# Images in DRAM with the two column parities side by side: blocks of columns in 2048-byte runs, blocks of rows in two DMAs

## The chip, the cores and the metric

The kernel runs on one core of a Trainium2 chip. The metric is the device time of one execution, from the first to the last instruction of the program, in microseconds (us). The time before is the median of three runs.

## The reference

Four layers work on images of 4 batches, 48 channels, 256 rows and 256 columns (float32). Each layer is `x = x + f(gn(x))`, where `gn` is a group norm with 16 groups of 3 channels.

```python
# layer 0
qkv = conv3x3_depthwise(conv1x1(gn(x), qkv_w), dw_w);  q, k, v = split(qkv)
x = x + conv1x1(softmax(l2n(q) @ l2n(k).T * temperature) @ v, proj_w)
# layers 1 and 2: four sweeps over the image, each one a chain of steps
D[t] = row[t] + conv1d(D[t-1], down_w)            # down, 256 steps
U    = the same weights, upwards over D           # up
R[t] = column[t] + conv1d(R[t-1], right_w)        # right
L    = the same upwards over R with left_w        # left
x = x + L
# layer 3
h = conv3x3_depthwise(conv1x1(gn(x), w_in), w_dw); x1, x2 = split(h)
x = x + filter_8x8_patches(conv1x1(gelu(x1) * x2, w_out), fft_w)
```

## The kernel before

An image (3,072 KB for each of 16 blocks, 48 MB in all) is stored in DRAM in sub-blocks. A block is 16 rows or 16 columns; a sub-block is the crossing of both, and it is stored by parity: `hp` is the parity of the row, `wp` that of the column, and 64 numbers (`SUB`) are left for one batch. The layout before is `[hb, wb, hp, wp, c, b, s]`: block of rows, block of columns, the two parities, channel, batch, the 64 numbers. One run of consecutive bytes for one channel is `(b s)`, 256 numbers or 1,024 bytes. This holds for the input `x` (the host writes it so) and for the four images `x1`, `x2`, `up` and `x3` between the layers.

In SBUF a block has 96 partitions, 48 channels times a parity, with 32 KB in each. For a block of rows (`row_block`) the partition is `(wp c)`, so the lower 48 partitions hold the even columns; for a block of columns (`col_block`) it is `(hp c)`. A block of rows is one DMA over all 96 partitions, 32 runs of 1,024 bytes in each. A block of columns is four DMAs, one for each `(hp, wp)`, over 48 partitions each, 16 runs of 1,024 bytes in each; first the two of partitions 0 to 47 (`hp` 0), then the two of 48 to 95. The phases of one batch (`RowStream`) load a block of rows of one batch in one DMA: 96 partitions, 32 runs of 256 bytes.

The phases follow each other with a barrier between them:

- `stats_phase` (st): loads the 16 blocks of rows of `x` into two tiles in turn, and VectorE takes their statistics. Nothing else runs. The load of block n + 2 is issued when VectorE is done with block n.
- `gram_phase` (qk), `value_phase` (va), `gated_phase` (gf): `RowStream` over 4 batches with 16 blocks of rows each. For each strip of 8 rows ScalarE writes `own_high`, GpSimd `own_low`, and SyncE (SP) issues two copies of each inside SBUF (`next_high`, `next_low`, one for 48 partitions each) that TensorE waits for. After every second strip SP issues the load of a later block; `value_phase` also stores a block of its result.
- `down_up_phase` (du, once for each of layers 1 and 2): blocks of rows in, the sweep down, lines stored; then the lines back in, the sweep up, blocks of rows out.
- `right_left_phase` (rl, twice): blocks of columns in, the sweep to the right, lines stored; then, going back for the sweep to the left, for each block: the lines in (3,072 KB), the block of the residual in, the block of the result out. In layer 2 ScalarE also writes the result again by patches (`repack`, L657), and SP stores it in eight DMAs a block (`store_patches`, L593). ScalarE may write a patch buffer again only when the store of two buffers before has landed (L663).
- `filter_phase` (fi).

All DMAs are issued by SP in the order in which its code is written, and they go through one queue. What waits for a load is written in semaphore counts: 16 for each DMA, so that `dve.wait_ge(loaded[k], 64 * i + 64)` waits for four.

Of the kernel before, what the change touches and what calls it, by code (L numbers as in the profile page):

```python
# [98 lines left out]
def stats_phase(nc, src, stats):  # L99

    with Phase(nc, "st") as ph:
# [5 lines left out]
        @block.sync  # L107
        def _(sp):
            for k in range(2):
                sp.dma_start(tiles[k][:, :].rearrange("p (k s) -> p k s", s=B * SUB),  # L110
                             row_block(src, k)).then_inc(loaded[k], 16)
            with sp.Fori(1, NB // 2) as i:
                for k in range(2):

                    ph.hold(sp, used, 2 * i + k - 1)
                    sp.dma_start(tiles[k][:, :].rearrange("p (k s) -> p k s", s=B * SUB),
                                 row_block(src, 2 * i + k)).then_inc(loaded[k], 16)
# [253 lines left out]
def down_up_phase(nc, src, taps, scale, shift, down, dst):  # L371
# [4 lines left out]
    with Phase(nc, "du") as ph:  # L376
# [13 lines left out]
        def _(sp):  # L390
            def load(n, k):
                sp.dma_start(wide[k][:, :].rearrange("p (k s) -> p k s", s=B * SUB), row_block(src, n))\
                  .then_inc(loaded[k], 16)
# [11 lines left out]
            def store_back(i, k):  # L405
                m = 2 * i + k
                ph.hold(sp, placed, BLK * m + BLK)
                sp.dma_start(row_block(dst, NB - 1 - m), wide[k][:, :].rearrange("p (k s) -> p k s", s=B * SUB))\
                  .then_inc(back_out[k], 16)
# [17 lines left out]
            for k in range(2):  # L427
                sp.wait_ge(back_out[k], 16 * (NB // 2))

        @block.scalar  # L430
        def _(act):
# [3 lines left out]
            def back(i, first=False):  # L435
                for k in range(2):
                    m = 2 * i + k
                    if not first:
                        act.wait_ge(back_out[k], 16 * i)
# [11 lines left out]
            with act.Fori(0, NB // 2) as i:  # L451
                for k in range(2):
                    act.wait_ge(loaded[k], 16 * i + 16)
# [80 lines left out]
def right_left_phase(nc, src, taps_right, taps_left, right, dst, residual, stats, patches=None):  # L534
# [4 lines left out]
    with Phase(nc, "rl") as ph:  # L539
# [16 lines left out]
        def pieces(t, n, tile):  # L556
            v4 = tile[:, :].rearrange("p (k q s) -> p k q s", q=2, s=B * SUB)
            return [(col_block(t, n, hp, wp), v4[hp * C:(hp + 1) * C, :, wp]) for hp in range(2) for wp in range(2)]

        @block.sync  # L560
        def _(sp):
            def load(n, k):
                for d, s in pieces(src, n, wide[k]):
# [5 lines left out]
            def load_residual(m):  # L569
                for d, s in pieces(residual, NB - 1 - m, results[m % 3]):  # L570
# [40 lines left out]
            for m in range(NB):  # L611
                if m >= 1:
                    store_back(m - 1)
                if m >= 2:
                    store_patches(m - 2, 3)
                    if m + 1 < NB:
                        sp.wait_ge(measured, m - 1)
                        sp.wait_ge(back_out[(m - 2) % 3], 64 * ((m - 2) // 3 + 1))
# [12 lines left out]
            for k in range(3):  # L631
                sp.wait_ge(back_out[k], 64 * len(range(k, NB, 3)))
# [56 lines left out]
        def _(dve):  # L689
            def there(i, first=False):  # L690
                for k in range(2):
                    n = 2 * i + k
                    dve.wait_ge(loaded[k], 64 * i + 64)
# [38 lines left out]
        def _(pool):  # L732
            def place(m, tile, count, first=False):
                pool.wait_ge(whole[tile], 64 * count + 64)
# [34 lines left out]
class RowStream:  # L769
# [83 lines left out]
    def norm(self, act, b, hb):  # L853
# [8 lines left out]
        self.ph.hold(act, self.raw_in[kr], 16 * self.loads_of(kr) * b + 16 * (hb // self.raws) + 16)  # L862
# [387 lines left out]
def value_phase(nc, src, scale, shift, w_v, dst, stats):  # L1250

    with Phase(nc, "va") as ph:
# [11 lines left out]
        def _(sp):  # L1264
            def store(b, hb):
                ph.hold(sp, added, 4 + NGB * b + 4 * (hb + 1))
                d = dst[hb][:, :, :, :, bass.ds(b, 1)].rearrange("wb hp wp c b s -> (wp c) (wb hp) (b s)")
                sp.dma_start(d, rs.raw[hb % 4][:, :].rearrange("p (k s) -> p k s", s=SUB)).then_inc(stored[hb % 4], 16)

            def before_load(b, hb):  # L1270
                if hb >= 2:
                    ph.hold(sp, stored[(hb - 2) % 4], 16 + 64 * b + 16 * ((hb - 2) // 4) + 16)
                    ph.hold(sp, measured, NB + NB * b + hb - 1)
                else:
                    ph.hold(sp, stored[hb + 2], 16 + 64 * b)
# [7 lines left out]
            for k in range(4):  # L1283
                sp.wait_ge(stored[k], 16 + 64 * B)
# [526 lines left out]
```

## Time and profile before

| | |
|---|---|
| median of 3 runs | 12107.07 us (12071.13, 12107.07, 12110.31) |
| profiled execution, its own time | 12072.02 us |
| its span | 12070.2 us |
| busy TensorE (PE) | 11062.8 us, 92% |
| busy VectorE, ScalarE, GpSimd | 7592.0, 3302.3, 5472.2 us |
| moved by DMA | 1907.40 MB, 1974004 packets |

PE is TensorE's matmuls and PEld its weight loads, DVE is VectorE, ACT ScalarE, POOL GpSimd; SPq, ACTq and so on are the sequencers of the engines, which issue DMAs and wait for semaphores. The profiled execution stands near the lowest of the three runs, 35 us below their median.

### The profile page before, as it was taken

What the parts mean: (1) busy time and instruction counts of PE and PEld (TensorE: products, weight loads), DVE (VectorE), ACT (ScalarE), POOL (GpSimd) and SP (SyncE); (2) the same over time, 40 slices, a digit from 0 to 9 for tenths busy, and PEclk for the clock granted to TensorE, in tenths of its full rate; (3) what the DMA queues carried; (4) which work ended last, traced back from release to release, by engine and by line L of the source; (5) the groups of instructions that cost most, each with busy time, mean ns of one, the idle gap of its engine ahead of it and who ended that gap; (6) DMA issues with size and microseconds to landing.
All of it is one profiled execution on the core that took longest, in us unless ns stands there. A gap on an engine that the chain in (4) does not pass through costs nothing. (4 is left out here: it accounts for less than half of the span.)

```text
span 12070.2 us, 242619 instructions
## 1 busy us (share of the span) xinstructions
PE 11062.8 (92%) x82492; PEld 10237.2 (85%) x82492; DVE 7592.0 (63%) x19405; ACT 3302.3 (27%) x3654; POOL 5472.2 (45%) x5025
## 2 busy tenths in 40 slices
PE   0999999899989998999899999999879999999999
PEld 0999999666669998998799889987779999999974
DVE  5444444322248886877778777866667676777754
ACT  0222222222222352023322450055622222222210
POOL 0666666333335554555455444544434444444410
PEclk9999999899999999999899999988889999999999
DMA  9666666699976567879765658799845555555569
GB/s 173 136 138 136 137 133 135 133 194 193 192 154 181 136 177 160 183 161 205 159 161 142 167 142 177 164 197 214 197 102 113 104 112 114 107 115 104 116 197 360
DMA packets 1974004, 1907.40 MB, mean 158 GB/s; under 512 B 1224122, under 2 KB 1863968, under 8 KB 1900960
## 3 DMA queue, kind: packets, MB, share of 16 engines
q1 hardware_dynamic: 1973152, 1897.01, 69.9%
q8 instruction: 417, 6.83, 0.2%
q14 instruction: 435, 3.56, 0.1%
HBM read 781.57 MB, written 578.81 MB: 113 GB/s over the span
## 5 line engine op out<-in xcount | busy, mean ns | idle before, releaser
L744 POOL TENSOR_TENSOR rl_wide<-rl_wide,rl_state 96x512 f32<-96x512 f32 x510 | 818.3, 1605 | 812.1 <-ACT rl_state L655 812.1
L273 PE MATMUL du_sum<-du_high,sw_down_high 96*96 96x256 f32 x6132 | 1085.8, 286 | 102.9 <-DVE du_high L335 75.7
L273 PE MATMUL du_sum<-du_low,sw_down_high 96*96 96x256 f32 x6132 | 1118.2, 291 | 0.1
L273 PE MATMUL du_sum<-du_high,sw_down_low 96*96 96x256 f32 x6132 | 1078.2, 284 | 0.0
L940 POOL TENSOR_TENSOR gf_own_low<-gf_sums,gf_own_high 96x2080 fp32r<-96x2080 f32 x128 | 598.5, 4676 | 901.4 <-DVE gf_hid_a L1520 896.4
L1436 PE MATMUL gf_four<-gf_own_high,l_w_hid_high 96*128 96x256 f32 x3072 | 883.8, 288 | 108.4 <-DMA gf_next_low<-gf_own_low 108.4
L273 PEld LDWEIGHTS du_sum<-du_high,sw_down_high 96*96 96x96 f32 x6132 | 831.9, 165 | 111.3 <-DVE du_high L335 78.8
L934 POOL TENSOR_TENSOR gf_sums<-gf_block 96x520 f32<-96x520 f32 x512 | 602.7, 1207 | 666.1 <-DVE gf_hid_a L1520 637.9
L940 POOL TENSOR_TENSOR qk_own_low<-qk_sums,qk_own_high 96x2080 fp32r<-96x2080 f32 x128 | 596.8, 4662 | 666.4 <-ACT qk_own_high L904 666.4
L1436 PE MATMUL gf_four<-gf_next_high,l_w_hid_low 96*128 96x256 f32 x3072 | 874.1, 285 | 0.0
L346 POOL TENSOR_TENSOR du_low<-du_state,du_high 96x128 fp32r<-96x128 f32 x1020 | 613.1, 601 | 573.2 <-DVE du_state L336 573.2
L1436 PE MATMUL gf_four<-gf_own_low,l_w_hid_high 96*128 96x256 f32 x3072 | 873.0, 284 | 0.0
L1436 PE MATMUL gf_four<-gf_next_low,l_w_hid_high 96*128 96x256 f32 x3072 | 872.9, 284 | 0.0
L1436 PE MATMUL gf_four<-gf_own_high,l_w_hid_low 96*128 96x256 f32 x3072 | 871.4, 284 | 0.0
L1436 PE MATMUL gf_four<-gf_next_high,l_w_hid_high 96*128 96x256 f32 x3072 | 871.4, 284 | 0.0
L346 POOL TENSOR_TENSOR du_low<-du_lines,du_high 96x128 fp32r<-96x128 f32 (+1 forms) x1024 | 614.9, 601 | 555.9 <-DVE du_lines L336 555.9
L346 POOL TENSOR_TENSOR rl_low<-rl_lines,rl_high 96x128 fp32r<-96x128 f32 (+1 forms) x1024 | 614.3, 600 | 550.4 <-DVE rl_lines L336 550.4
L273 PEld LDWEIGHTS du_sum<-du_high,sw_down_low 96*96 96x96 f32 x6132 | 831.9, 164 | 0.0
L273 PEld LDWEIGHTS du_sum<-du_low,sw_down_high 96*96 96x96 f32 x6132 | 796.1, 164 | 31.5 <-issue 0.8
L1155 DVE COPY qk_second<-qk_four 128x192 f32<-128x192 f32 x512 | 183.0, 357 | 1008.5 <-PE qk_four L1128 1008.5
L648 ACT COPY rl_sum<-rl_lines 96x512 f32<-96x512 f32 x510 | 304.5, 597 | 1846.3 <-PE rl_sum L282 1846.0
L449 ACT COPY du_wide<-du_state 96x512 f32<-96x512 f32 x510 | 626.4, 1228 | 558.7 <-DVE du_state L336 558.7
(214 smaller groups left out, 32209.2 us busy)
## 6 DMA issues: line engine op xcount, KB each, us to landing
qk_next_high<-qk_own_high SPq DMA_DIRECT2D x256, 389.8 KB, 5.2
qk_next_low<-qk_own_low SPq DMA_DIRECT2D x256, 389.8 KB, 5.3
gf_next_high<-gf_own_high SPq DMA_DIRECT2D x256, 389.8 KB, 5.4
gf_next_low<-gf_own_low SPq DMA_DIRECT2D x256, 389.8 KB, 5.5
du_wide<-x SPq DMA_DIRECT2D x32, 3072.0 KB, 17.0
up<-du_wide SPq DMA_DIRECT2D x32, 3072.0 KB, 20.9
rl_wide<-up SPq DMA_DIRECT2D x128, 768.0 KB, 15.8
rl_wide<-x SPq DMA_DIRECT2D x128, 768.0 KB, 16.5
```

The source lines that it names most:

```text
L273: mm = self.nc.tensor.matmul(self.half_line(r, c), w[0:kk, k, :], x[0:kk, (r - 1) % RING, 2 * c:2 * c + 2, k:k + PAIRS], start=(n == 0 and ...
L346: self.nc.gpsimd.tensor_tensor(self.low_of(r, 2 * c, nb), state[:, 0:nb], self.high_of(r, 2 * c, nb), ALU.subtract)\
L449: nc.scalar.copy(result(k, r), by_sub_block(state[:, (TURN + r) % DEPTH])).then_inc(placed, 1)
L648: nc.scalar.copy(ch.line(t), lines[n % 2][:, at].rearrange("p b n -> p (b n)")).then_inc(ch.filled, 1)
L744: nc.gpsimd.tensor_tensor(at, at, by_sub_block(row), ALU.add).then_inc(placed, 1)
L934: last = g.tensor_tensor(self.sums4[:, 4 * t:4 * t + 4, :], d[x], d[y], op)
L940: g.tensor_tensor(self.parts["own", "low"][u % SLOTS][:, :, :], rows, self.parts["own", "high"][u % SLOTS][:, :, :], ALU.subtract).then_in ...
L1155: nc.vector.tensor_copy(second[:, 0, :], m[2]).then_inc(mid, 1)
L1436: mm = nc.tensor.matmul(four[tile][t // 2][:, (t % 2) * HN:(t % 2 + 1) * HN], w[:, ab, t, 128 * tile:128 * tile + 128], px[:, 4 * t + 2 * ...
```

## The change

The layout in DRAM becomes `[hb, c, wb, hp, wp, b, s]`: the channel moves outwards, and the two column parities stand next to each other. A block of columns has then runs of `(wp b s)`, 2,048 bytes, and is moved in two DMAs, one for each half of the partitions. A block of rows can no longer be written as one pattern over `(wp c)`, and is moved in two DMAs, `wp` 0 into partitions 0 to 47 and `wp` 1 into 48 to 95, with runs of 1,024 bytes as before, 2,048 bytes apart; so are the blocks of one batch, with runs of 256 bytes. The semaphore counts follow. What stands in SBUF, and what the engines compute, is the same.

```diff
-def row_block(t, hb):
-    return t[hb].rearrange("wb hp wp c b s -> (wp c) (wb hp) (b s)")
-def col_block(t, wb, hp, wp):
-    return t[:, wb, hp, wp].rearrange("hb c b s -> c hb (b s)")
+def row_block(t, hb, tile):
+    v = tile[:, :].rearrange("p (k s) -> p k s", s=B * SUB)
+    return [(t[hb][:, :, :, wp].rearrange("c wb hp b s -> c (wb hp) (b s)"), v[wp * C:(wp + 1) * C]) for wp in range(2)]
+def row_part(t, hb, b, tile):
+    v = tile[:, :].rearrange("p (k s) -> p k s", s=SUB)
+    return [(t[hb][:, :, :, wp, bass.ds(b, 1)].rearrange("c wb hp b s -> c (wb hp) (b s)"), v[wp * C:(wp + 1) * C])
+            for wp in range(2)]
+def col_block(t, wb, tile):
+    v = tile[:, :].rearrange("p (k x) -> p k x", k=NB)
+    return [(t[:, :, wb, hp].rearrange("hb c wp b s -> c hb (wp b s)"), v[hp * C:(hp + 1) * C]) for hp in range(2)]
...
-                    sp.dma_start(tiles[k][:, :].rearrange("p (k s) -> p k s", s=B * SUB),
-                                 row_block(src, 2 * i + k)).then_inc(loaded[k], 16)
+                    for d, v in row_block(src, 2 * i + k, tiles[k]):
+                        sp.dma_start(v, d).then_inc(loaded[k], 16)
...
-                    dve.wait_ge(loaded[k], 16 * i + 16)
+                    dve.wait_ge(loaded[k], 32 * i + 32)
...
-        def pieces(t, n, tile):
-            v4 = tile[:, :].rearrange("p (k q s) -> p k q s", q=2, s=B * SUB)
-            return [(col_block(t, n, hp, wp), v4[hp * C:(hp + 1) * C, :, wp]) for hp in range(2) for wp in range(2)]
...
-                for d, s in pieces(residual, NB - 1 - m, results[m % 3]):
+                for d, s in col_block(residual, NB - 1 - m, results[m % 3]):
                     sp.dma_start(s, d).then_inc(whole[m % 3], 16)
...
-                for d, s in pieces(dst, NB - 1 - m, results[m % 3]):
+                for d, s in col_block(dst, NB - 1 - m, results[m % 3]):
                     sp.dma_start(d, s).then_inc(back_out[m % 3], 16)
...
-        d = self.raw[k][:, :].rearrange("p (k s) -> p k s", s=SUB)
-        s = self.src[hb][:, :, :, :, bass.ds(b, 1)].rearrange("wb hp wp c b s -> (wp c) (wb hp) (b s)")
-        sp.dma_start(d, s).then_inc(self.raw_in[k], 16)
+        for s, d in row_part(self.src, hb, b, self.raw[k]):
+            sp.dma_start(d, s).then_inc(self.raw_in[k], 16)
...
-    dram = {n: nc.dram_tensor(n, [NB, NB, 2, 2, C, B, SUB], F32).ap() for n in ("x1", "x2", "up", "x3")}
+    dram = {n: nc.dram_tensor(n, [NB, C, NB, 2, 2, B, SUB], F32).ap() for n in ("x1", "x2", "up", "x3")}
```

What this makes of SP's queue is read at three places. A row is one instruction with its line, output, input and the shape of what it moves (partitions x runs x numbers in a run); `x2` is a count. The first place is the loop of `stats_phase`, before:

```order
L112 ISA
L116 ISA
L116 DMA st_tile<-in_x 96x32x256
L74 REGISTER_ALU
L116 ISA
L116 DMA st_tile<-in_x 96x32x256
```

and with the change:

```order
L126 DMA st_tile<-in_x 48x32x256
L126 ISA
L126 DMA st_tile<-in_x 48x32x256
L74 REGISTER_ALU
L126 ISA
L126 DMA st_tile<-in_x 48x32x256
L126 ISA
L126 DMA st_tile<-in_x 48x32x256
```

Each load of 96 partitions has become two of 48, one behind the other. The second place is SP in `value_phase`, between the copies of one strip and those of the next, before:

```order
L839 DMA va_next_low<-va_own_low 48x1299
L74 ISA x2
L812 ISA
L812 DMA va_raw<-in_x 96x32x64
L74 ISA
L838 DMA va_next_high<-va_own_high 48x1299
```

and with the change:

```order
L843 DMA va_next_low<-va_own_low 48x1299
L74 ISA x2
L816 ISA
L816 DMA va_raw<-in_x 48x32x64
L816 ISA
L816 DMA va_raw<-in_x 48x32x64
L74 ISA
L842 DMA va_next_high<-va_own_high 48x1299
```

The copy of the next strip stands behind two loads in place of one, with the same bytes. The third place is SP in the second `right_left_phase`, one block of the way back, before:

```order
L584 DMA x<-rl_wide 48x16x256 x4
L593 DMA patches<-rl_px 48x16x128 x2
L571 DMA rl_wide<-x 48x16x256 x4
L593 DMA patches<-rl_px 48x16x128 x4
L579 DMA rl_lines<-right 96x8192
L593 DMA patches<-rl_px 48x16x128 x2
```

and with the change:

```order
L589 DMA x<-rl_wide 48x16x512 x2
L598 DMA patches<-rl_px 48x16x128 x2
L576 DMA rl_wide<-x 48x16x512 x2
L598 DMA patches<-rl_px 48x16x128 x4
L584 DMA rl_lines<-right 96x8192
L598 DMA patches<-rl_px 48x16x128 x2
```

Result and residual move in two DMAs each, with runs of 512 numbers; the order among the DMAs is the same.

## Rows read from the trace of the kernel before

**Rows 1.** The page: busy time by engine, share of the span, instructions.

```profile
PE 11062.8 (92%) x82492; PEld 10237.2 (85%) x82492; DVE 7592.0 (63%) x19405; ACT 3302.3 (27%) x3654; POOL 5472.2 (45%) x5025
```

**Rows 2.** Waits of the whole span: waiter, awaited, us in total, times, longest.

```profile
DVE all_stats L134 <- DMA st_tile<-in_x: 99.8, 16, 18.2
...
ACT rl_px L666 <- DMA patches<-rl_px: 148.2, 28, 15.3
...
PE va_sum L1313 <- DMA va_next_high<-va_own_high: 77.0, 45, 20.7
```

**Rows 3.** Timeline of `stats_phase`: start, us, instruction, idle before it.

```profile
103.04 9.59 DVE L134 BATCH_NORM_STATS2 all_stats<-st_tile 96x512 f32 x16 [5.41 <-DMA st_tile<-in_x]
118.12 9.59 DVE L134 BATCH_NORM_STATS2 all_stats<-st_tile 96x512 f32 x16 [5.49 <-DMA st_tile<-in_x]
```

**Rows 4.** Windows (from:to, length, busy by engine; then clock, DMA share, GB/s).

```profile
100.00:220.00 120.00, 0.00 (x0) 0.00 (x0) 76.71 (x128) 0.00 (x0) 0.00 (x0) 1.00 1.13 211
4658.00:4668.00 10.00, 4.04 (x18) 3.81 (x18) 0.00 (x0) 0.00 (x0) 1.25 (x3) 0.67 1.15 123
4670.00:4675.00 5.00, 0.00 (x0) 0.00 (x0) 0.00 (x0) 0.00 (x0) 0.00 (x0) 0.50 1.13 220
5252.00:5258.00 6.00, 6.00 (x47) 5.35 (x46) 3.63 (x9) 2.81 (x6) 3.24 (x2) 1.00 1.13 132
8332.00:8343.00 11.00, 11.00 (x48) 9.66 (x46) 5.14 (x12) 5.17 (x7) 4.56 (x3) 0.50 1.04 239
293.00:297.00 4.00, 0.00 (x0) 0.00 (x0) 0.00 (x0) 1.31 (x2) 0.00 (x0) 1.00 1.35 180
2292.00:3390.00 1098.00, 1037.92 (x4275) 691.87 (x4274) 314.24 (x483) 320.17 (x357) 356.15 (x119) 0.98 0.95 194
```

**Rows 5.** Windows with stores alone: 1,024-byte runs of rows, lines, and columns.

```profile
4120.50:4126.50 6.00, 6.00 (x51) 5.92 (x50) 4.72 (x14) 3.00 (x4) 3.45 (x6) 1.00 1.09 386
3557.00:3563.00 6.00, 6.00 (x52) 5.91 (x50) 4.79 (x14) 5.38 (x3) 3.20 (x6) 1.00 0.99 426
5299.00:5302.00 3.00, 3.00 (x25) 2.68 (x24) 2.55 (x6) 1.40 (x4) 1.62 (x1) 1.00 1.07 348
```

**Rows 6.** Timeline of `value_phase`: SP's issues, then TensorE.

```profile
2504.36 0.61 SPq L812 DMA_DIRECT2D va_raw<-in_x  x1
2507.15 1.80 SPq L838 DMA_DIRECT2D va_next_high<-va_own_high  x1
...
2515.18 0.95 PE L1313 MATMUL va_sum<-va_own_high,va_w_high 96*96 96x512 f32 x3 [0.95 <-DMA va_next_high<-va_own_high]
```

**Rows 7.** Second `right_left_phase`, way back: SP's load of lines, once a block.

```profile
7876.24 0.32 SPq L579 DMA_DIRECT2D rl_lines<-right  x1
7920.14 0.33 SPq L579 DMA_DIRECT2D rl_lines<-right  x1
...
8619.55 0.33 SPq L579 DMA_DIRECT2D rl_lines<-right  x1
```

**Rows 8.** The same stretch in windows: one block, then twelve.

```profile
7877.00:7920.00 43.00, 43.00 (x315) 37.81 (x314) 32.83 (x75) 27.05 (x40) 25.84 (x16) 1.00 0.71 178
7920.00:8620.00 700.00, 637.91 (x3861) 563.10 (x3860) 441.03 (x967) 412.90 (x579) 307.23 (x192) 0.80 0.99 216
```

**Rows 9.** Timeline of one block there: a step of TensorE that waits for ScalarE, which waits for patches.

```profile
8385.18 1.06 ACT L666 COPY rl_px<-rl_wide 96x512 f32<-96x512 f32 x1 [6.34 <-DMA patches<-rl_px]
...
8386.85 0.95 PE L273 MATMUL rl_sum<-rl_high,sw_left_high 96*96 96x256 f32 x3 [3.70 <-ACT rl_sum L648]
```

**Rows 10.** First loads of a `down_up_phase` and a `right_left_phase`: issue, and the first work.

```profile
3478.32 61.79 SPq L392 DMA_DIRECT2D du_wide<-x  x3
3496.01 8.05 ACT L456 ACTIVATE du_wide<-du_wide,all_shift,all_scale 96x2048 f32<-96x2048 f32 x4 [27.04 <-DMA du_wide<-x]
4655.07 25.13 SPq L564 DMA_DIRECT2D rl_wide<-up  x8
4677.71 0.42 DVE L335 TENSOR_TENSOR rl_high<-rl_sum,rl_wide 96x256 fp32r<-96x256 f32 x1 [39.45 <-DMA rl_wide<-up]
```

More of the change, by code:

```diff
@@ L109, in _ @@
             for k in range(2):
-                sp.dma_start(tiles[k][:, :].rearrange("p (k s) -> p k s", s=B * SUB),
-                             row_block(src, k)).then_inc(loaded[k], 16)
+                for d, v in row_block(src, k, tiles[k]):
+                    sp.dma_start(v, d).then_inc(loaded[k], 16)
             with sp.Fori(1, NB // 2) as i:
@@ L391, in load @@
             def load(n, k):
-                sp.dma_start(wide[k][:, :].rearrange("p (k s) -> p k s", s=B * SUB), row_block(src, n))\
-                  .then_inc(loaded[k], 16)
+                for d, v in row_block(src, n, wide[k]):
+                    sp.dma_start(v, d).then_inc(loaded[k], 16)
             def store(n, k):
@@ L407, in store_back @@
                 ph.hold(sp, placed, BLK * m + BLK)
-                sp.dma_start(row_block(dst, NB - 1 - m), wide[k][:, :].rearrange("p (k s) -> p k s", s=B * SUB))\
-                  .then_inc(back_out[k], 16)
+                for d, v in row_block(dst, NB - 1 - m, wide[k]):
+                    sp.dma_start(d, v).then_inc(back_out[k], 16)
             load(0, 0)
@@ L438, in back @@
                     if not first:
-                        act.wait_ge(back_out[k], 16 * i)
+                        act.wait_ge(back_out[k], 32 * i)
                     for r in range(BLK):
@@ L452, in _ @@
                 for k in range(2):
-                    act.wait_ge(loaded[k], 16 * i + 16)
+                    act.wait_ge(loaded[k], 32 * i + 32)
                     v = wide[k][:, :].rearrange("p (k b s) -> p k b s", b=B, s=SUB)
@@ L562, in load @@
             def load(n, k):
-                for d, s in pieces(src, n, wide[k]):
+                for d, s in col_block(src, n, wide[k]):
                     sp.dma_start(s, d).then_inc(loaded[k], 16)
@@ L631, in _ @@
             for k in range(3):
-                sp.wait_ge(back_out[k], 64 * len(range(k, NB, 3)))
+                sp.wait_ge(back_out[k], 32 * len(range(k, NB, 3)))
             if patches is not None:
@@ L733, in place @@
             def place(m, tile, count, first=False):
-                pool.wait_ge(whole[tile], 64 * count + 64)
+                pool.wait_ge(whole[tile], 32 * count + 32)
                 for r in range(BLK):
@@ L861, in norm @@
         raw = self.raw[kr][:, :].rearrange("p (k q i j) -> p k q i j", k=NB, q=2, i=HALF)
-        self.ph.hold(act, self.raw_in[kr], 16 * self.loads_of(kr) * b + 16 * (hb // self.raws) + 16)
+        self.ph.hold(act, self.raw_in[kr], 32 * self.loads_of(kr) * b + 32 * (hb // self.raws) + 32)
         if hb:
@@ L1266, in store @@
                 ph.hold(sp, added, 4 + NGB * b + 4 * (hb + 1))
-                d = dst[hb][:, :, :, :, bass.ds(b, 1)].rearrange("wb hp wp c b s -> (wp c) (wb hp) (b s)")
-                sp.dma_start(d, rs.raw[hb % 4][:, :].rearrange("p (k s) -> p k s", s=SUB)).then_inc(stored[hb % 4], 16)
+                for d, v in row_part(dst, hb, b, rs.raw[hb % 4]):
+                    sp.dma_start(d, v).then_inc(stored[hb % 4], 16)
             def before_load(b, hb):
                 if hb >= 2:
-                    ph.hold(sp, stored[(hb - 2) % 4], 16 + 64 * b + 16 * ((hb - 2) // 4) + 16)
+                    ph.hold(sp, stored[(hb - 2) % 4], 32 + 128 * b + 32 * ((hb - 2) // 4) + 32)
                     ph.hold(sp, measured, NB + NB * b + hb - 1)
                 else:
-                    ph.hold(sp, stored[hb + 2], 16 + 64 * b)
+                    ph.hold(sp, stored[hb + 2], 32 + 128 * b)
                     ph.hold(sp, measured, NB + NB * b + hb - 1)
```

14 lines of the change are left out of this document (7 added, 7 removed).

## The prediction

> **What bounds the kernel now.** I read the page first: TensorE is busy for 92% of the span, VectorE for 63%, and no other engine for more than half [rows 1]. The change touches nothing but DMAs, so it can only act where a DMA ends a wait of the critical engine. The list of waits names three such places [rows 2]: VectorE waits for the tile in `stats_phase` (99.8 us, 16 times), TensorE waits for `va_next_high` in `value_phase` (77.0 us, 45 times), and ScalarE waits for the patch stores in the second `right_left_phase` (148.2 us, 28 times). I looked at each in the timeline and in windows.
>
> *Stats.* VectorE needs 9.59 us for a block and then idles 5.4 to 5.5 us until the next tile lands; a block starts every 15.1 us [rows 3]. In the window of 100 to 220 us the DMA share is 1.13 (packets overlap, so a full queue reads over 1) at 211 GB/s [rows 4]. A block has 3.146 MB, and 3.146 / 0.211 = 14.9 us: the stage is bound by the load.
>
> *Value.* SP issues the load of a block at 2504.36 and the next `next_high` copy at 2507.15; TensorE starts on that strip at 2515.18, after 0.95 us of waiting [rows 6]. The copy takes 8 us because it stands in the queue behind the load. Leaving out the longest wait (20.7, the start), 56.3 us remain in 44 waits.
>
> *Second way back to the left.* SP's load of the lines marks the blocks: 43.9 us from 7876.24 to 7920.14, then 12 blocks in 699.4 us, 58.3 us each [rows 7]. In the first of these stretches the granted clock is 1.00 and the DMA share 0.71; in the second 0.80 and 0.99 at 216 GB/s [rows 8]. One block shows the chain: ScalarE waits 6.34 us for a patch store, then TensorE has waited 3.70 us for ScalarE [rows 9]. So 14.4 us of each of 12 blocks hang on a full queue; part of them is TensorE at the lower of its two clocks (1.2 GHz) after such waits. The first way back has no patches and no such wait in the list.
>
> **What the halves of a block cost.** A load of columns already comes in halves: partitions 0 to 47, then 48 to 95. With 1,024-byte runs the first half moves at 123 and 132 GB/s in two windows, the second at 220 [rows 4]. Per block that is 1.573 / 0.127 = 12.4 us and 1.573 / 0.220 = 7.15 us, 19.5 us in all. Undivided, the load of rows with the same runs takes 14.9 us. Two things differ between them: the halves, and the addresses (the runs of one channel lie 3 MB apart in DRAM for columns, 96 KB for rows). That both halves have the same pitch and differ by 220 against 127 says that the partitions matter; how much of the rest is pitch, no row tells.
>
> Stores show no such thing: 386 GB/s for rows, 348 for columns, 426 for the lines with their long runs [rows 5]. I cost the split of stores at nothing.
>
> **Term 1, stats, +40 us.** Each block of rows becomes two half loads, 2 KB apart in DRAM. Upper bound: 19.5 - 14.9 = 4.6 us for each of 16 blocks, +74. Lower bound: the best rate of a 96-partition load in this trace, the lines at 239 GB/s [rows 4], 13.2 us, -1.7 x 16 = -27. I take +2.5 us a block, a little over half of the upper bound, since the halves stay and the 3 MB pitch goes: 16 x 2.5 = +40. VectorE's idle time of 5.4 us is where it appears, growing to about 8. Nothing covers it.
>
> Here a rule speaks. The Trainium skill (SBUF — State Buffer, section "Door 1: The DMA port swizzle") says that partitions 0 to 63 reach only 8 of 16 ports, at about 27.2 GB/s each. The lower 48 partitions put 8 on each of four of these ports, the upper 48 put 4 on each of twelve; an estimate from the page is 9.6 and 4.8 us, 14.4 us a block, and the term would be -8 us by it. The trace agrees with the direction (127 against 220 GB/s) and not with the size (163 and 326 by the page).
>
> **Term 2, value, +36 us.** The load of one batch and block, 0.786 MB in 256-byte runs, runs at 180 GB/s [rows 4], 4.37 us. If halves cost the same share as in term 1, it becomes 4.37 x 17.4 / 14.9 = 5.10 us, +0.73. The copy behind it lands as much later. There were 44 waits and little slack in the other blocks; I count 50 of 64 blocks, +36 us. Bounds: with 19.5 / 14.9 the load grows by 1.35 us, x 60 = +81; at 13.2 / 14.9 it shrinks by 0.5, x 44 = -22. The second issue costs SP 0.6 us, and between the load's issue and the next copy's there are 2.8 [rows 6]: covered. Stores are split too; the next copy follows later still. In `gram_phase` and `gated_phase` the same delay exists, but there TensorE does not wait for copies except at starts.
>
> **Term 3, first loads, +3 us.** At each phase's start the first block is exposed: 3478.32 to 3496.01 for rows, 4655.07 to 4677.71 for columns [rows 10]. Two `down_up` starts x 2.5 = +5; two `right_left` starts x -2.3 (term 4) = -4.6; three `RowStream` starts x 0.7 = +2. Bounds -10 to +10.
>
> **Term 4, second way back, -34 us.** A block loads 3.146 MB of residual and stores 3.146 MB of result in columns, now with 2,048-byte runs. For the load the bounds are nothing (19.5 us), and the same 13.2 us, -6.3. I take -2.3: the long-run store against the short-run store is 426 to 386 or 348, 10 to 20%, and 2,048 bytes should give over half of that. For the store: 3.146 / 0.348 = 9.0 us, 5% off, -0.5; bounds 0 and -1.6 (426 GB/s). Sum -2.8 us x 12 blocks = -34, bounds 0 and -95. The block's floor is 43.9 us, 14.4 below, so all of it counts as long as the queue is full. Whether the clock comes back with the shorter wait is open; I add nothing for it.
>
> **Hidden.** The remaining blocks of columns and rows (both sweeps down and up, to the right, the first way back) move behind chains of steps that wait for no DMA; column blocks get shorter, row blocks longer by 2.5 to 4.6 us in some 44 us a block. Cost nothing. The last drains: -1.
>
> **Sum.** 40 + 36 + 3 - 34 - 1 = +44 us, on the profiled execution's own time of 12072.0: 12116. That execution is 35 us under the median of the three runs (12107.07), with one more run at the same low place (12071.13) and one at the high (12110.31). Against the median it would be 12151. I put the time between, at 12134.
>
> **Rivals.**
>
> *A. The DRAM pitch made the column loads slow, not the halves.* Then halves at close addresses together take no longer than the undivided load. For: the two column loads are the only ones with a 3 MB pitch, and the upper half at 220 GB/s is slower than a long-run load over more partitions at 239. Against: the lower half is slow at the same pitch. Worked out: row blocks stay at 14.9 us, so stats and value change by nothing; column blocks come down to the same 14.9, which gives starts 2 x -4.6 = -9 and the second way back 12 x (-4.6 - 0.5) = -61; together -70: 12002 by own time, 12020 in the middle as above. It decides from where the two halves of a row load take less than about 15.5 us together. This one ends faster. By its own rule on ports the Trainium skill (SBUF — State Buffer, the same section) would have it so, with 14.4 us a block. Chance 0.20.
>
> *B. Both sides shrink.* The value phase takes the longer load in the slack of its queue (term 2 near +10), stats +25, second way back -30: within 36 us of nothing, 12090 to 12110. For: in the value phase the share of DMA is 0.95 on average, while a full queue of 256-byte loads reads 1.35 [rows 4]. Chance 0.25.
>
> *C. The full price of halves.* Stats +74, value +81, starts +8, second way back -12 (2,048-byte runs gain nothing in the loads, the hot half sets their time): +151, 12241. For: the rates of the halves are measured with the same partitions. Chance 0.13.
>
> *D. A pitch of 64 KB between channels collides in DRAM.* Then every row load suffers: at half the 211 GB/s stats alone grow by 16 x 14.9 = +238. Against: the lines have 512 KB between channels in DRAM and move at 239 and 426 GB/s [rows 4, 5]. Chance 0.03.
>
> That the change would not do what it says is excluded by SP's order: 48x16x512 in two DMAs.
>
> **How the numbers follow.** My forecast (slower by about 0.4%) has 0.39, A 0.20, B 0.25, C 0.13, D 0.03. About 0.3% (36 us) is what a measurement of this kernel can tell from no change. Slower: 0.39 + 0.13 + 0.03 = 0.55, less 0.03 of the forecast's own lower edge: 0.52. Same: 0.25 + 0.03 = 0.28. Faster: 0.20. The range leaves out a good third of A and half of C with D: 12005 to 12225. The forecast's own range is 12095 to 12180.
>
> **What would show it.** In the changed profile: VectorE's idle time before each block of `stats_phase` at about 8 us (forecast), 5 to 6 (A), 10 (C); windows in stats whose rate alternates between a low and a high value; TensorE's waits for `va_next_high` near 110 us; the blocks of the second way back at 55 to 56 us (forecast), 53 (A) or 57 to 58 (C). The prediction is wrong if a half load of rows runs far from 127 and 220 GB/s, or if the shorter queue lets TensorE's clock stay at 2.4 GHz on the second way back, which would give more than the 2.8 us a block that I count.

## The result, and the profile after

The changed kernel takes 12251.73 us in the median of 5 runs (12208.14 to 12304.93), the kernel before 12107.07 (12071.13 to 12147.27): ratio 1.0118, interval 1.0077 to 1.0159, slower by 145 us. I had forecast 12134, with 12225 as the upper end. The profiled execution has a span of 12249.6 us.

The page of the changed kernel, busy time by engine, beside [rows 1]:

```profile
PE 11107.3 (91%) x82492; PEld 10271.5 (84%) x82492; DVE 7593.4 (62%) x19405; ACT 3302.2 (27%) x3654; POOL 5471.3 (45%) x5025
```

TensorE is busy 44.5 us longer with the same instructions (part of them at its lower clock), while the span grew by 179.4: most of the loss is idle time. The waits name the place. Those that answer to [rows 2], and one more:

```profile
DVE all_stats L143 <- DMA st_tile<-in_x: 175.1, 16, 23.2
...
ACT rl_px L671 <- DMA patches<-rl_px: 142.0, 25, 16.6
...
PE va_sum L1317 <- DMA va_next_high<-va_own_high: 104.8, 41, 23.2
...
DVE rl_high L344 <- DMA rl_wide<-up: 85.0, 2, 43.0
```

VectorE waits 75.3 us longer in `stats_phase`, TensorE 27.8 us longer for the copies in `value_phase`, and the patches are where they were. VectorE waits 85.0 us for the first blocks of the two `right_left` phases; it was 77.0 before. The timeline of the stats stage after the change, beside [rows 3]:

```profile
86.84 9.59 DVE L143 BATCH_NORM_STATS2 all_stats<-st_tile 96x512 f32 x16 [9.89 <-DMA st_tile<-in_x]
106.61 9.59 DVE L143 BATCH_NORM_STATS2 all_stats<-st_tile 96x512 f32 x16 [10.18 <-DMA st_tile<-in_x]
```

A block takes 19.8 us instead of 15.1, VectorE idles 10 us before each. Windows of the changed kernel say why. The columns are those of [rows 4]: the stats stage as a whole, a lower half and an upper half in it, a lower and an upper half of columns with their new 2,048-byte runs, the value stage, and the twelve blocks of the second way back:

```profile
100.00:220.00 120.00, 0.00 (x0) 0.00 (x0) 55.28 (x93) 0.00 (x0) 0.00 (x0) 1.00 1.14 157
...
107.00:111.00 4.00, 0.00 (x0) 0.00 (x0) 4.00 (x8) 0.00 (x0) 0.00 (x0) 1.00 1.14 120
...
99.00:103.00 4.00, 0.00 (x0) 0.00 (x0) 0.00 (x0) 0.00 (x0) 0.00 (x0) 1.00 1.13 215
...
4812.00:4820.00 8.00, 8.00 (x56) 7.95 (x55) 5.28 (x16) 0.00 (x0) 3.62 (x7) 0.79 1.08 127
4826.00:4829.00 3.00, 3.00 (x27) 2.97 (x26) 2.50 (x8) 0.00 (x0) 1.69 (x3) 1.00 1.09 216
...
2340.00:3560.00 1220.00, 1125.68 (x4544) 752.07 (x4545) 330.60 (x508) 344.77 (x381) 379.36 (x127) 0.95 0.98 185
...
8083.00:8793.00 710.00, 641.81 (x3860) 566.51 (x3860) 440.85 (x968) 413.96 (x577) 307.17 (x193) 0.78 0.95 214
```

Rows in halves run at 120 and 215 GB/s, about the rates of the column halves before (123, 132 and 220), though the runs of one channel lie 2 KB apart in a row block (and the channels 64 KB), while they lie 3 MB apart in a column block. Columns with runs twice as long run at 127 and 216: no faster.

The first loads, beside [rows 10]: SP's issue and the first work that needs the data.

```profile
3603.06 19.98 SPq L402 DMA_DIRECT2D du_wide<-x  x4
3625.53 8.05 ACT L465 ACTIVATE du_wide<-du_wide,all_shift,all_scale 96x2048 f32<-96x2048 f32 x4 [32.41 <-DMA du_wide<-x]
...
4788.40 11.69 SPq L569 DMA_DIRECT2D rl_wide<-up  x4
...
4810.85 0.42 DVE L344 TENSOR_TENSOR rl_high<-rl_sum,rl_wide 96x256 fp32r<-96x256 f32 x1 [42.96 <-DMA rl_wide<-up]
```

Rows 22.5 us instead of 17.7. Columns 22.5 instead of 22.6; but VectorE has idled 42.96 us before them instead of 39.45, because the last store of `down_up`, which SP waits for, takes longer. SP issues that store, and then the first load of columns: before, with the change, and with halves in the old layout (E13 below):

```profile
4639.51 0.32 SPq L408 DMA_DIRECT2D up<-du_wide  x1
...
4769.14 4.08 SPq L418 DMA_DIRECT2D up<-du_wide  x2
...
4753.62 3.68 SPq L412 DMA_DIRECT2D up<-du_wide  x2
4771.87 5.22 SPq L568 DMA_DIRECT2D rl_wide<-up  x4
```

To the load that follows it is 15.6 us (4655.07), 19.3 us (4788.40) and 18.3 us.

The first issue of each phase divides the span; stats is counted from the start of the span. Each column below is a stage in us: stats, qk with the gram, value, down-up 1, right-left 1, down-up 2, right-left 2, gated; then the mean block of the twelve on the second way back (first and last load of the lines, divided) and their median. The runs E1 to E14 are told below:

```
                            stats    qk   value   du1    rl1    du2    rl2   gated   block mean, median
before                      288.5 1963.2 1226.6 1176.8 1365.6 1229.6 1568.8 2831.7   58.3  57.8
after                       363.8 1964.6 1274.7 1185.3 1384.7 1240.2 1581.3 2835.6   59.1  57.0
E1  stats halves            357.8 1964.6 1222.6 1176.0 1382.3 1230.6 1604.5 2831.9   60.7  58.2
E2  after, two queues       297.7 1975.1 1270.2 1185.9 1388.4 1238.7 1623.4 2834.2   62.0  58.0
E3  stats cut at 32         248.2 1958.9 1218.8 1177.0 1378.9 1230.7 1600.3 2831.1   61.5  58.5
E4  after, columns in four  349.2 1963.5 1275.2 1186.2 1390.1 1240.6 1598.4 2835.0   61.0  57.9
E5  stream loads halves     288.0 1972.8 1261.8 1177.8 1432.5 1232.6 1584.8 2835.4   59.6  58.2
E6  value stores halves     288.7 1959.0 1227.2 1176.4 1376.6 1228.3 1612.6 2833.8   62.2  58.6
E7  rows cut at 32          249.9 1963.8 1240.5 1175.7 1398.9 1228.5 1581.3 2831.4   59.4  57.5
E8  rows, lines cut at 32   249.5 1963.6 1241.2 1175.2 1378.8 1214.0 1547.6 2831.4   56.2  54.5
E10 stats, du, lines cut    250.7 1965.3 1218.3 1177.2 1369.6 1214.1 1550.5 2834.9   57.8  55.7
E11 lines alone             287.4 1961.6 1220.0 1176.7 1394.1 1215.5 1520.2 2834.3   55.4  54.6
E12 stream loads by block   287.8 1967.2 1210.6 1177.2 1365.8 1233.1 1565.3 2834.7   58.9  58.1
E13 all rows halves, old    360.0 1968.0 1260.2 1183.7 1388.7 1237.6 1566.3 2837.6   58.1  57.6
E14 E10 and by block        250.5 1966.6 1215.2 1176.0 1395.8 1213.5 1572.1 2830.8   59.0  54.8
```

Where code is the same, value and down-up repeat within some 8 us, and stats as well where its loads are whole or cut at 32; in halves it scatters by 15 (349.2 to 363.8). The right-left stages do not: rl1 with unchanged code runs from 1365.6 to 1432.5 and rl2 from 1565.3 to 1612.6, since on their ways back single blocks take 65 to 78 us in one run and not in the next; one such block of E6, 75.7 us long, had a granted clock of 0.53, the two behind it, 56.3 and 56.6 us long, 0.88 and 0.87. The median block is the steadier reading. In these terms the change costs 75 in stats, 48 in value, 19 in the two down-up stages and 5 in qk and gated, 148 us, close to the 145 between the medians; the 32 us of the right-left stages in this one profile are within their scatter.

### The profile page after: what moved, and what is told of

It reads as the page before. It is cut to its first block and busy times, and to the rows that moved or that the text cites. A ratio compares the mean times of both kernels' runs of the same rounds, so it can differ in the third digit from the quotient of the medians.

```text
span 12249.6 us, 243231 instructions
## 1 busy us (share of the span) xinstructions
PE 11107.3 (91%) x82492; PEld 10271.5 (84%) x82492; DVE 7593.4 (62%) x19405; ACT 3302.2 (27%) x3654; POOL 5471.3 (45%) x5025
## 6 DMA issues: line engine op xcount, KB each, us to landing
rl_wide<-up SPq DMA_DIRECT2D x64, 1536.0 KB, 20.5
```

## The experiments

**E1: only the stats loads in halves, old layout.**

```
-sp.dma_start(tiles[k][:, :]..., row_block(src, n)).then_inc(loaded[k], 16)
+for lo, hi in ((0, C), (C, C2)):
+    sp.dma_start(tiles[k][lo:hi, :]..., row_block(src, n)[lo:hi]).then_inc(loaded[k], 16)
```

> The kernel before, its DRAM layout unchanged; only the loads of stats_phase come as two DMAs, partitions 0 to 47 and 48 to 95, in runs of 1,024 bytes as ever. Theory 1 (the halves cost: a DMA into partitions 0 to 47 alone runs at about 125 GB/s, one into 48 to 95 at about 215): the stage from its first load to the first load of the next phase grows from 288.5 us by the same 75 us as with the change (363.8), VectorE waits some 175 us for the tile instead of 99.8, and the windows alternate between about 125 and 215 GB/s. The whole kernel is about 75 us slower. Rival (the new layout costs: the pitch of 64 KB between channels, or the 2 KB between the halves of a block, slows DRAM): the stage stays within 10 us of 288.5 and the windows read 211 GB/s throughout.

Stats 357.8 us, 69 more than before; ratio of the whole kernel 1.0044 (1.0029 to 1.006), 35 to 73 us. VectorE in this run:

```profile
105.38 9.59 DVE L136 BATCH_NORM_STATS2 all_stats<-st_tile 96x512 f32 x16 [9.83 <-DMA st_tile<-in_x]
```

The halves alone give 69 of the 75 us, and the four profiles with halved stats loads on one queue (349.2 to 363.8) scatter by more than what is left. The new layout has no part in it that shows.

**E2: the changed kernel, upper halves of stats issued on ScalarE's queue.**

```
-for d, v in row_block(src, n, tiles[k]): sp.dma_start(v, d)
+block.sync: the pair's [0]; block.scalar: the pair's [1], with the same waits
```

> The changed kernel; only in stats_phase the upper half of each block (partitions 48 to 95) is issued by ScalarE's queue instead of SP's, so that both halves are under way together. Theory 1 (each half by itself cannot use all of the paths into the SBUF: 48 low partitions share few of them; nothing is lost if the other half runs at the same time): a block takes no more than the undivided load of the kernel before, 14.9 us, perhaps 12 to 14, and the stage comes down from 363.8 to 290 us or less. Rival (the number of descriptors or the smaller DMA is what costs, whatever runs beside it): the block stays at 19 us or more, the stage above 350. In between would mean that both halves share one limit that the low partitions set (1.573 MB at 127 GB/s, 12.4 us, hides the upper half entirely: 12.4 us a block, the same as theory 1 in its weaker form).

Stats 297.7 in the one execution of this kernel, a little over the 290 that I had set: side by side the same half loads cost within 9 us of what the undivided loads cost. So a half is not slow by its number of descriptors; it is slow when no other half runs beside it.

**E3: stats loads cut at partition 32, old layout.** As E1 with `((32, C2), (0, 32))`.

> The kernel before, its DRAM layout unchanged; only the loads of stats_phase come as two DMAs, cut at another place: partitions 32 to 95 first, then 0 to 31. Theory 1 (which partitions a DMA covers sets its rate; the two halves of the change are an unlucky cut, and partitions 0 to 31 by themselves are no worse than 0 to 47): the rate differs from both the undivided load and the halves; if 32 to 95 is spread evenly over the paths into the SBUF, a block takes 11.5 to 12.5 us instead of 14.9 and the stage shrinks by 35 to 55 us (VectorE's own 9.6 us a block is the floor). Rival (dividing a load costs as such, by the second DMA or its descriptors): the block takes more than 14.9 us and the stage more than 288.5 us, up to the 75 us of the halves.

Stats 248.2, 40 us under before; ratio 0.9973 (0.9959 to 0.9986). Dividing a load is no cost as such; where it is cut decides the sign.

**E4: the changed kernel, columns again in four DMAs with 1,024-byte runs.**

```
-[(t[:, :, wb, hp].rearrange("hb c wp b s -> c hb (wp b s)"), v[hp * C:(hp + 1) * C]) for hp in range(2)]
+[(t[:, :, wb, hp, wp].rearrange("hb c b s -> c hb (b s)"), v[hp * C:(hp + 1) * C, :, wp]) for hp ... for wp ...]
```

> The changed kernel; only the blocks of columns go back to four DMAs with runs of 1,024 bytes (two column parities apart), in the new DRAM layout; rows stay as changed. Theory 1 (a run of 2,048 bytes gains nothing in these loads and stores, as the traces of before and after suggest: 125 and 215 GB/s at either length): both right-left stages stay within 10 us of the changed kernel's (1384.7 and 1581.3), about 59 us a block on the second way back, and the whole time stays within 0.3%. Rival (the longer run is worth the 2 to 3 us a block that I predicted, and something else ate it): the second way back is 25 to 40 us longer than with the change, near 61 to 62 us a block.

Ratio to before 1.0124 (1.0091 to 1.0157), as with the change; rl2 17 us longer than in the profile of the change, which is scatter, as the median block tells: 57.9 us, where the changed column code has 57.0 and, in E2, 58.0. The longer run brings nothing on the way back that can be told: profiles with unchanged columns have medians from 57.5 to 58.6.

**E5 and E6: the value stage's loads alone, and its stores alone, in halves, old layout.** The loop of E1 in `RowStream.load`, and in the store of `value_phase`.

> The kernel before; only the loads of RowStream (the raw rows of qk, value and gated phase) come in the two halves 0 to 47 and 48 to 95; the stores of value_phase stay whole. In the changed kernel the value stage grew by 48 to 51 us (three runs). Theory 1 (my term 2: the halved load in front of the next_high copy delays it): the value stage, from its first load to the first load of down_up, grows by 35 to 50 us over the 1219 to 1227 us of the kernels with whole loads. Rival (the halved stores carry it, which I had costed at nothing): it grows by less than 15 us. The stages of qk and gated stay as they are in both cases.

> The kernel before; only the stores of value_phase go out in the two halves 0 to 47 and 48 to 95; all loads stay whole. Theory 1 (stores from the SBUF lose nothing by the halves, as I assumed): the value stage stays within 6 us of 1219 to 1227 us. Rival (stores in halves are slower as well; the last drain of down_up took 16 us instead of 12 in the changed kernel, about 200 instead of 270 GB/s): it grows by 10 to 35 us.

One execution each. Loads: 1261.8, 40 us over the mean of the unchanged code (1221). Stores: 1227.2, within scatter. So the greater part of term 2 belongs to the loads.

**E7 and E8: all row loads cut at 32; then the loads of the lines too.**

> The kernel before, its DRAM layout unchanged; every load of rows (stats, the raw rows of qk, value and gated, both down_up sweeps) is cut into partitions 32 to 95 and 0 to 31. Theory 1 (the same cut that took the stats stage from 288.5 to 248.2 us helps wherever a row load stands in the way): stats 248; the value stage shorter by 10 to 40 us, since the copy behind the load of 0.786 MB lands earlier; first loads of down_up shorter by 2 to 4 us each; the whole 55 to 85 us faster than before. Rival (with 256-byte runs the number of descriptors sets the time, not the partitions): the value stage stays within 6 us or grows by the second issue, and the whole gain is that of stats alone, 30 to 40 us.

> As the kernel in which all row loads are cut into 32 to 95 and 0 to 31, and the loads of the lines (both ways back) cut the same way. Theory 1 (the second way back to the left is set by a full queue, 14.4 us a block above its floor of 43.9, so whatever shortens a transfer in it shortens the block): the lines take 10.5 to 12 us instead of 13.2, each of 12 blocks gets 1 to 2.5 us shorter, 12 to 30 us less in the second right-left stage. Rival (the block is set by the patch stores and ScalarE's order of work, not by the sum of the transfers): no change in that stage beyond its spread of 20 us between runs of the same code, the block stays at 58 to 59 us.

E7: ratio 0.9981 (0.9962 to 1.0001); stats 249.9 as in E3, but the value stage 1240.5, 19 longer than with whole loads: the first theory is wrong there. TensorE waits 81.0 us for `va_next_high` there (77.0 before, 71.4 in E3, where the value stage is unchanged) and is busy 1128.22 us (1121.68 and 1118.12) with the same matmuls. E8: 0.9944 (0.9926 to 0.9963); its median block is 54.5 us against 57.5 and down-up 2 is 14 us shorter (down-up 1, with the same edit, is not; that stays open).

**E9: the transfers alone.** The kernel leaves out all computation. A phase of eight blocks for each form, three in flight.

> Not the kernel but its transfers alone, one phase for each form, with nothing else running: eight (sixteen for the first) blocks of 3.146 MB, three in flight, from the input or to the output; all computation is left out and the output holds ones. Theory 1 (which partitions a DMA covers sets its rate, wherever the runs lie in DRAM and whether they have 1,024 or 2,048 bytes): rows whole about 14.9 us a block (211 GB/s); rows in halves 19.5 to 20 us in the layout of before and in the new one alike; halves on two queues 12.5 to 15; the cut at partition 32 11.5 to 12.5; columns in 1,024-byte and in 2,048-byte runs both 19.5; lines whole 13.2, in halves 17 to 19, cut at 32 10.5 to 11.5; stores of rows whole 8 to 11 us, in halves 3 to 5 us more. For the raw rows with 256-byte runs (0.786 MB): whole 4.4, halves 5.1 to 5.7, cut at 32 3.5 to 4.4. Rival for the columns (the pitch of 3 MB between the runs of a channel, or their length, counts): the two forms of columns differ by more than 1 us a block, or the halves of rows in the new layout differ from the halves in the old one by that much.

The windows of it, one in the steady part of each phase (columns: from:to, length, GpSimd's busy time, clock, DMA share, GB/s). In order: stores of rows whole, in halves, cut at 32, columns of 1,024 and of 2,048 bytes, lines whole; loads of rows whole, halves in the old and in the new layout, two queues, cut at 32; columns of 1,024 and of 2,048 bytes; raw rows whole, halves, cut at 32; lines whole, halves, cut at 32.

```profile
60.00:200.00 140.00, 0.00 (x0) 1.00 0.84 256
270.00:350.00 80.00, 0.00 (x0) 1.00 0.93 238
400.00:470.00 70.00, 1.58 (x1) 1.00 0.95 271
510.00:600.00 90.00, 0.66 (x1) 1.00 0.90 232
640.00:720.00 80.00, 0.00 (x0) 1.00 0.94 256
770.00:820.00 50.00, 0.00 (x0) 1.00 0.89 273
870.00:940.00 70.00, 0.00 (x0) 1.00 1.12 209
1000.00:1090.00 90.00, 0.00 (x0) 1.00 1.13 167
1150.00:1240.00 90.00, 0.00 (x0) 1.00 1.13 172
1300.00:1380.00 80.00, 0.00 (x0) 1.00 1.12 219
1420.00:1490.00 70.00, 0.00 (x0) 1.00 1.12 237
1530.00:1620.00 90.00, 0.00 (x0) 1.00 1.13 174
1680.00:1770.00 90.00, 0.00 (x0) 1.00 1.07 167
1815.00:1840.00 25.00, 0.00 (x0) 1.00 1.20 175
1853.00:1883.00 30.00, 0.00 (x0) 1.00 1.43 165
1895.00:1920.00 25.00, 0.00 (x0) 1.00 1.14 184
1950.00:2010.00 60.00, 0.00 (x0) 1.00 1.01 220
2070.00:2160.00 90.00, 0.00 (x0) 1.00 1.01 171
2215.00:2275.00 60.00, 0.00 (x0) 1.00 0.99 291
```

A block of 3.146 MB divided by these rates: rows whole 15.1 us, in halves 18.8 and 18.3, on two queues 14.4, cut at 32 13.3; columns 18.1 and 18.8; lines 14.3, 18.4 and 10.8. In halves, neither the layout (167 and 172 GB/s) nor the run length (columns 174 and 167, the long runs of the lines 171) moves a load by more than 4%. The partitions move it by up to 70% (lines, 171 to 291). With the cut at 32 the run length does count: 237 for rows, 291 for lines. The raw rows are too short for their windows: over the whole of each phase that cut gains them nothing that can be told. Whole, in halves, cut at 32:

```profile
1809.70:1844.80 35.10, 0.00 (x0) 1.00 1.20 179
1847.00:1885.30 38.30, 0.00 (x0) 1.00 1.38 164
1887.90:1923.90 36.00, 0.00 (x0) 1.00 1.08 175
```

Inside two of these phases, piece by piece: partitions 32 to 95 and 0 to 31; then 0 to 47 and 48 to 95:

```profile
1440.50:1444.50 4.00, 0.00 (x0) 1.00 1.11 348
1446.00:1450.00 4.00, 0.00 (x0) 1.00 1.12 206
...
1010.00:1020.00 10.00, 0.00 (x0) 1.00 1.13 133
1024.00:1028.00 4.00, 0.00 (x0) 1.00 1.12 207
```

A load into the 32 partitions 0 to 31 moves 206 GB/s, one into the 48 partitions 0 to 47 moves 133, and one into the 48 partitions 48 to 95, of the same shape, 207. So it is not their number that sets the rate, but which they are. The Trainium skill (SBUF — State Buffer, "Door 1: The DMA port swizzle") has the mapping: partition p and p + 32 share a port up to 63, and 64 to 95 use the other eight. By it 0 to 31 put four on each of eight ports, 0 to 47 eight on four of them, 32 to 95 four on each of sixteen; an estimate from its 27.2 GB/s a port is 218, 163 and 435. The trace has 206, 133 and 348: the order is the page's, the sizes are 6 to 20% lower. For 48 to 95 and for all 96 partitions an estimate from the same figure is 326 each, and the trace has 207 and 209, 36% lower. So the mapping fits the slow piece and the cut, but not all pieces, and that the ports are the cause is not shown; that the partitions are is.

**E10: stats, down-up and lines loads cut at 32, raw rows whole.**

> The kernel before, DRAM layout unchanged; stats, down_up loads and the loads of the lines cut into partitions 32 to 95 and 0 to 31; the raw rows of qk, value and gated phase stay whole, since the value stage grew by 18 us when they were cut so. By the stages of the earlier runs: stats -40, first loads of down_up -2, lines -40 to -60, value 0: 85 to 105 us faster than the kernel before, 12005 to 12025 us. Rival (the gain of the lines is the scatter of the clock in the right-left stages): 12060 or more.

12014.23 us where before took 12121.67: ratio 0.9912 (0.9893 to 0.9932). The time is in the range that the stages of the earlier runs gave.

**E11: the lines' loads alone cut at 32.**

> The kernel before; only the loads of the lines on the ways back (up and left, both layers) come as two DMAs, partitions 32 to 95 and 0 to 31. The kernel with rows and lines cut was 60 us faster than the one with rows alone. Theory 1 (on the second way back to the left the queue is full, so a transfer shortened by 1.7 to 2.7 us shortens each of 12 blocks by as much, and some of TensorE's time at the lower clock goes with it): 30 to 60 us faster than before, the second right-left stage near 1550 us instead of 1569 to 1613, its block at 54 to 57 us. Rival (nothing hangs on the lines' load): within 15 us of before.

Ratio 0.9967 (0.9949 to 0.9985), some 40 us; rl2 at 1520.2 is the shortest of all, down-up 2 at 1215.5. SP's loads of lines in this run, beside [rows 7]:

```profile
7925.20 1.16 SPq L581 DMA_DIRECT2D rl_lines<-right  x2
7979.66 1.15 SPq L581 DMA_DIRECT2D rl_lines<-right  x2
8034.57 1.60 SPq L581 DMA_DIRECT2D rl_lines<-right  x2
```

54.5 and 54.9 us a block, with a median of 54.6 instead of 57.8: 3.2 us less, and the load alone got 14.3 - 10.8 = 3.5 us shorter in E9. The waits for patch stores fall as well, from 148.2 to 112.9 us. The block of the second way back is indeed set by its transfers.

**E12: raw rows in two DMAs of all 96 partitions, by column blocks.**

```
-sp.dma_start(d, s).then_inc(self.raw_in[k], 16)
+for lo, hi in ((0, NB), (NB, 2 * NB)): sp.dma_start(d[:, lo:hi], s[:, lo:hi]).then_inc(self.raw_in[k], 16)
```

> The kernel before; each load of RowStream (raw rows of qk, value and gated phase) comes as two DMAs of all 96 partitions, the first with the eight column blocks on the left, the second with the rest: as many DMAs as with the halves, but every one covers all partitions. The value stage took 1261.8 us with the loads in partition halves, 1240 with the cut at partition 32 and 1219 to 1227 with whole loads. Theory 1 (the second DMA itself costs there, by its issue on SP's queue and its descriptors, and explains the 18 us of the cut at 32, which is no slower by itself): 1235 to 1245 us here. Rival (only the partitions count; the cut at 32 delays the copies in another way): 1219 to 1229 us.

Value 1210.6 in its one execution: a second DMA costs nothing there, and the first theory falls.

**E13: every row load and store in halves, old layout, old columns.**

> The kernel before with its DRAM layout and its blocks of columns unchanged, but every load and store of rows (stats, raw rows, value stores, both down_up loads and stores) in the two halves 0 to 47 and 48 to 95: all that the change does to rows, without the layout. Theory 1 (the halves are the whole of the slowdown; layout and 2,048-byte column runs do nothing): 12240 to 12265 us where the kernel before takes 12110 to 12120, ratio 1.010 to 1.013, with stats 350 to 364, value 1270 to 1275, both down_up stages 9 to 10 us longer. Rival (the layout has a part of its own): less than 1.008 and the missing part shows in one of these stages.

Ratio 1.0121 (1.0095 to 1.0147). The kernel with halves and without the layout is as slow as the changed one. By stages it is not all the same: stats 360.0 is as expected, value 1260.2 is 10 us under the lower end of what I had expected, and the down-up stages are 7 and 8 us longer than before instead of 9 to 10.

**E14: E10 with the raw rows by column blocks.**

> The fastest kernel so far (DRAM layout of before; stats, down_up and lines loads cut into partitions 32 to 95 and 0 to 31, 12014 us where before took 12122, ratio 0.9912) with one more edit: the raw rows of qk, value and gated phase come as two DMAs of all 96 partitions each, by column blocks, which gave a value stage of 1210.6 us where whole loads gave 1218 to 1227. Theory 1 (a shorter DMA in front of the copies makes them land earlier; worth some 8 to 12 us): ratio 0.989 to 0.991, value stage 1207 to 1214. Rival (that single stage was scatter): the value stage is back at 1218 to 1227 and the ratio at 0.9912.

Ratio 0.9917 (0.9891 to 0.9943), value 1215.2: no gain over E10 in the whole time that can be told. Both profiles with this edit have a shorter value stage than any with whole loads (1218.3 at the least), so that 3 to 8 us of gain stay open.

## Why the prediction was too low

**Term 1, stats: +40 forecast, +75 measured (61 to 75 in the four profiles); the failed step.** The place and the mechanism were right, the size was not: the step that failed is the choice of 2.5 us a block. I had the bound, 19.5 - 14.9 = 4.6 us a block or +74, from the same partitions in the same trace, and took "a little over half of the upper bound, since the halves stay and the 3 MB pitch goes". The pitch was worth nothing: halves of rows in the old layout, where the runs of one channel lie 96 KB apart, in the new one, where they lie 2 KB apart, and columns, 3 MB apart, all run at 167 to 174 GB/s (E9), and E1 has the loss without the layout. My sum was +44, the stages give +148: this step is 35 of the 104 us between them (term 2 is 12, term 3 is 17, term 4 is 34, and qk and gated, which I had costed at nothing, 5). Rival A died with the pitch.

**The rule on ports.** Of the Trainium skill's rule (SBUF — State Buffer, "Door 1: The DMA port swizzle") I had said that it is right in direction and not in size. That held; but I had used it only as a rate for the halves at hand. Its mapping also says that the cut matters: an estimate from its ports is 9.6 us for a block cut at 32, the same 9.6 for an undivided one, and 14.4 for the halves. In E9 they take 13.3, 15.1 and 18.8 us. So the trace agrees that the halves are the worst; the 1.8 us that the cut at 32 gains over the undivided load, and with it the 40 us of E3, the rule does not give.

**Term 2, value: +36 forecast, +48 measured.** The loads give it (E5, +40), the stores alone nothing (E6). The whole stage as a window, before and after, shows the part that I had left out:

```profile
2251.00:3478.00 1227.00, 1121.68 (x4612) 748.11 (x4612) 350.31 (x537) 347.99 (x386) 387.42 (x131) 0.96 0.91 187
...
2328.00:3603.00 1275.00, 1142.20 (x4612) 763.16 (x4612) 350.31 (x537) 348.88 (x386) 386.83 (x131) 0.94 0.96 180
```

TensorE is busy 20.5 us longer for the same 4,612 matmuls, at a granted clock of 0.94 instead of 0.96. With the 27.8 us of waiting for copies that is the 48 us. The copies' delay alone is thus less than the +36 that I had forecast for it, and the lower clock, which I had counted nowhere, makes up for it and more; that the longer waits bring the lower clock is argued, not shown. With halves in the old layout the stage takes 1260 to 1262 (E5, E13), with the change 1270 to 1275 (three profiles): some 12 us may belong to the new layout. No run isolates it.

**Term 3, first loads and drains: +2 forecast, +19 in the down-up stages.** The first load grew by 4.8 and 5.7 us, not 2.5, by the same error as term 1. And the stores were costed at nothing: the last row store of each stage holds up the next phase by 3.7 and 3.3 us more. In E9, with three blocks under way, halves of rows store at 238 GB/s, whole ones at 256; that is 0.9 us a block, so most of the longer drain of a store that stands alone is not explained. The 386 GB/s of [rows 5] were no sustained rate of a row store.

**Term 4, second way back: -34 forecast, nothing measured; the second failed step.** "2,048 bytes should give over half of that" carried the gain of long runs from stores to loads. Loads do not have it: 174 and 167 GB/s in E9 for the short and the long run, 127 and 216 for the halves in the changed kernel. Stores do, 232 to 256. By these rates a block gains 1.3 us in the store and loses 0.8 in the load, an estimate of -6 us for twelve blocks, less than the scatter of the stage. The other half of the step, that all of a shortened transfer counts while the queue is full, was right, and E11 shows it with a transfer that really got shorter.

**The rivals.** C, "the full price of halves", with stats +74 and starts +8, is nearly what happened; its total of +151 is close to 145 partly by chance, since its value term of +81 was too high and the drains were missing from it. It had 0.13. Two of its signs came, 10 us of idle time in stats and a block near 57 us; the third, waits for `va_next_high`, came out at 104.8 us, near the forecast's 110. I had argued for the middle of a range whose upper end came from the same partitions and whose lower end came from other ones. B and D did not happen: the value stage did not swallow the longer load, and 64 KB between channels cost no row load its rate.

**Left open.** Why the cut at 32 costs 19 us in the value stage (E7, E8), where the load by itself is hardly slower (175 against 179 GB/s over whole phases of E9). Some 7 to 10 us of it are busy time of TensorE. Something in its order against the copies may do it; E12 only speaks against the second DMA as such. Why the new layout's value stage is some 12 us longer than that with halves alone, and why the last store of a stage loses more by its halves than stores in E9, stays open too.

## What to carry to other kernels

Before a DMA is divided, or a layout chosen that forces a division, look in the trace for a transfer with exactly the partitions of the new pieces and take its rate whole; for loads in halves, its address pattern and its run length from 1 KB up mattered here by 4% or less. Partitions 0 to 47 were the slowest piece of all, and with runs of 1 KB or more 32 to 95 with 0 to 31 beats the undivided load (237 against 209 GB/s, 291 against 220). Where a queue is full, nearly every us off a transfer is a us off the block (3.2 of 3.5), so look first at which DMA in it is cheapest to shorten: here the lines, at no change of layout.

## What was unexpected in the hardware

- A DMA into partitions 0 to 31 ran faster in total (206 GB/s) than one into 0 to 47 (133), and 32 to 95 at 348 where all 96 had 209.
- Two slow halves at once, on two queues, reach 219 GB/s, the rate of the undivided load.
- The cut at 32 gained most with long runs: lines 220 to 291, rows with 1,024-byte runs 209 to 237, 256-byte runs nothing (179 and 175 over whole phases).
- Runs of 2,048 instead of 1,024 bytes gave stores 10% (232 to 256) and loads nothing (174 to 167).
